# Expert tiles of a mixture-of-experts layer: SyncE reads the row numbers of four pairs of tiles at once

## The reference

```python
x = x + xattn(layernorm(x), ...)
h = layernorm(x)
probs = softmax(h @ router_weight.T)
topv, topi = top_k(probs, 4); topv = topv / sum(topv)
g = einsum('th,ehf->etf', h, w_gate)       # 32 experts, 256 -> 96
u = einsum('th,ehf->etf', h, w_up)
out = einsum('te,etf,efh->th', combine, silu(g) * u, w_down)
shared = silu(h @ sw_gate) * (h @ sw_up) @ sw_down   # 256 -> 512 -> 256
x = x + out + sigmoid(h @ sgate_w) * shared
```

## Time and profile before

| | us |
|---|---|
| three timed runs | 517.47, 515.96, 512.97 |
| their median | 515.96 |
| the profiled execution, its span | 667.5 |
| TensorE busy in the span | 574.4 (86%) |
| VectorE busy | 363.5 (54%) |
| ScalarE busy | 288.7 (43%) |
| GpSimd busy | 269.4 (40%) |
| start of SP's first read of `tile_row` | 302.9 |
| start of the last transfer to `loaded` | 566.2 |

### The profile page before, as it was taken

The page is one execution under the profiler, slowest core; times in us unless marked ns, Lnnn a source line. Parts: engine busy times, 40 slices in busy tenths (PEclk is TensorE's granted clock), DMA queues, the critical chain, the costliest instruction groups (busy, mean ns, idle before and its releaser), DMA issues. The chain is left out here.

```text
span 667.5 us, 13365 instructions
## 1 busy us (share of the span) xinstructions
PE 574.4 (86%) x3945; PEld 478.3 (72%) x3945; DVE 363.5 (54%) x1199; ACT 288.7 (43%) x719; POOL 269.4 (40%) x344
## 2 busy tenths in 40 slices
PE   8998787788887777899998988778877898979998
PEld 7997777677777565677886666656666676658886
DVE  5575455555555351565553635445454444536998
ACT  5775444555444440613463545444454544401111
POOL 1004444445555458380034544445454454560000
PEclk9999788987778788699997977988989978989999
DMA  5573544444433322293145444544444544228996
GB/s 160 181 227 128 170 156 129 144 134 145 138 123 113 110 76 107 70 244 98 31 130 148 131 140 124 140 136 139 130 140 140 150 131 132 87 86 330 368 340 230
DMA packets 65956, 100.77 MB, mean 151 GB/s; under 512 B 9856, under 2 KB 52864, under 8 KB 65792
## 3 DMA queue, kind: packets, MB, share of 16 engines
q1 hardware_dynamic: 48704, 60.30, 30.6%
q0 software_dynamic: 12672, 35.41, 14.7%
q10 hardware_dynamic: 4512, 4.23, 1.9%
HBM read 55.92 MB, written 43.97 MB: 150 GB/s over the span
## 5 line engine op out<-in xcount | busy, mean ns | idle before, releaser
L512 POOL DMA_INDIRECT returned<-arena,back x136 | 130.6, 960 | 171.7 <-DVE back L1629 81.5
L481 POOL DMA_INDIRECT sent<-rows,slot x128 | 129.9, 1015 | 159.2 <-issue 82.7
L1100 PE MATMUL bank<-w_gu,arena 128*128 x416 | 94.7, 363 | 26.6 <-issue 16.6
L1100 PEld LDWEIGHTS bank<-w_gu,arena 128*128 128x128 f32 x416 | 73.0, 205 | 32.8 <-issue 32.8
L1580 DVE TENSOR_TENSOR arena<-bank,arena 128x192 f32<-128x192 f32 x68 | 24.2, 356 | 113.5 <-ACT arena L737 94.5
L737 ACT ACTIVATE arena<-bank 128x192 f32<-128x192 f32 x68 | 22.3, 329 | 127.0 <-remote 70.5
L806 PE MATMUL bank<-w_hi_all,att_split 128*128 128x256 f32 x256 | 56.8, 314 | 18.6 <-issue 18.6
L1597 DVE TENSOR_SCALAR arena<-bank,back_to 128x256 f32<-128x256 f32 x136 | 59.0, 476 | 6.3 <-remote 5.3
L806 PE MATMUL bank<-att_split,w_hi_all 128*128 128x256 f32 x256 | 55.5, 336 | 1.4 <-issue 1.3
L710 ACT COPY hnt<-w_gu 128x384 f32 x128 | 55.7, 509 | 0.0
L806 PEld LDWEIGHTS bank<-w_hi_all,att_split 128*128 128x128 f32 x256 | 42.4, 208 | 18.2 <-issue 18.2
(11 more groups left out here) (216 smaller groups left out, 1128.6 us busy)
## 6 DMA issues: line engine op xcount, KB each, us to landing
arena<-returned SPq DMA_DIRECT2D x16, 1024.0 KB, 7.2
loaded<-sent SPq DMA_DIRECT2D x104, 134.0 KB
w_gu<-w_gate_up SPq DMA_DIRECT2D x32, 192.0 KB
sent<-rows SPq DMA_DIRECT2D x4, 1072.0 KB, 6.2
loaded<-sent SPq DMA_DIRECT2D x128, 33.5 KB
resid<-x SPq DMA_DIRECT2D x16, 256.0 KB, 2.9
att_plain<-ctx_t SPq DMA_DIRECT2D x16, 256.0 KB, 3.1
out<-resid ACTq DMA_DIRECT2D x7, 512.0 KB, 4.9
```

The lines of the kernel that those rows point to most:

```text
L481: pool.indirect_dma_start(out=sent, out_offset=bass.IndirectOffsetOnAxis(ap=slot[:, 2 * b + j, k:k + 1], axis=0), in_=rows[:, u, j, :], in ...
L512: pool.indirect_dma_start(out=returned, out_offset=bass.IndirectOffsetOnAxis(ap=back[:, t:t + 1], axis=0), in_=down_e[u][:, s, :], in_offs ...
L1100: last = pe.matmul(view[:, s, :], rows_t[:, s, c, :], w_gu[:, c, bass.ds(e[s - 2 + len(e)], 1), :] .rearrange("p e f -> p (e f)"), start=( ...
```

## The change

SP reads at pairs 0, 4, 8 and so on with one instruction the row numbers of that pair and the three behind it: eleven values at pairs 0 and 64, fourteen at the others. Seventeen reads in place of 68. The registers are kept until their pairs' transfers are issued. The transfers, their waits and their order stay. The bound given to the compiler for the value, which is used for no check at run time, is now the same for all pairs.

```diff
             for pair in range(pairs):
-                u = pair % RING
-                first, size = column_of(pair), QUARTER if mixed(pair) else P
-                _, at = nc.values_load_multi_w_load_instructions(
-                    tile_row[0:1, first:first + (5 if mixed(pair) else 2)], engines=[mybir.EngineType.SP],
-                    min_val=0, max_val=EXPERTS * tokens - size,
-                    skip_runtime_bounds_check_because="a tile's first row is a row of an expert's "
-                                                      "region, at most its count less a tile on")
+                u, size = pair % RING, QUARTER if mixed(pair) else P
+                if pair % 4 == 0:
+                    first = column_of(pair)
+                    _, rows_at = nc.values_load_multi_w_load_instructions(
+                        tile_row[0:1, first:first + sum(5 if mixed(p) else 2 for p in range(pair, pair + 4))],
+                        engines=[mybir.EngineType.SP], min_val=0, max_val=EXPERTS * tokens - QUARTER,
+                        skip_runtime_bounds_check_because="a tile's first row is a row of an expert's "
+                                                          "region, at most its count less a tile on")
+                at = rows_at[column_of(pair) - first:]
                 wait(sp, "turned_psum", pair - RING + 1)
                 wait(sp, "back_ready", (pair - RING) // 2 + 1)
                 for q in range(P // size):
```

## The result

| | before | after |
|---|---|---|
| median of 11 runs each, us | 515.96 | 511.17 |
| lowest to highest, us | 510.08 to 519.54 | 510.09 to 512.86 |
| ratio, 95% interval | | 0.9917 (0.9889 to 0.9945) |

The change makes the kernel faster by 0.8% (4.3 us by the ratio, 4.8 us between the medians). That is less than 1%, but the interval of the ratio leaves out 1. The fastest runs of the two are equal, but on the side of the kernel before this is one run of 11; the next is 512.97. In a later set none of its 19 runs is under 513.43 us, and the changed kernel's eight are at 510.31 to 513.22.

The account below looks back on a forecast made before the run. TensorE was taken to bound the stage of 68 expert pairs, with SP's reads hidden by its lead; 0 us removed and 0 us added on the path left 516 us at 516, range 511 to 521.

Parts of the forecast that it names:

- within 1%: Whole kernel: timed result less than about 1%, 5 us, from no change; chance 0.85.
- The price of a read: SP's queue: 200 ns a value, 69 ns fixed, about half from columns divisible by four; reads 46.9 us before, 46.5 after.
- SP's load is equal and under TensorE's: Expert stage, four pairs: SP 10.4 to 11.0 us before, 10.8 after; TensorE 12.2 us.
- The clean stretch is the hardest on SP: Expert stage, 336.7 to 352 us: TensorE sets the pace, 3.06 us a pair, leaving SP least time; model of timed runs.
- some four pairs: Ring of six tiles: SP is this far ahead of TensorE, which hides later transfers; without it, 29 us.
- the half with the read: SP, two of four pairs: 6.6 us against 6.1 for two pairs, so pair 4k at most 0.5 us behind its release.
- The 42.2 us of waiting of SP: SP waits for DVE's slot lists at L1629, 18 times: the supplier waits for its customers, not they for it.
- The first rival, a late pair 4k: Long read makes pair 4k late, TensorE waits at L1049 once in four pairs; 524 us, up to 545; chance 0.08.
- The second rival, tiles that come earlier: Reads have a fixed price, tiles come earlier: 513 us, or 506 to 509 with unseen waits; gain over 1%: chance 0.08.

Follow-up runs that it names:

- aligned8: The changed kernel with groups of eight pairs beginning at pairs 7, 15, 23 and a first group of seven, 9 reads; 510.97 us, 0.9887 of the kernel before.
- first trace: Profile of the unchanged kernel before that the prediction used, at the slow level; it spans 667.5 us.
- second trace: New profile of the unchanged kernel before, at the 515 us level; it spans 512.7 us, timed median 514.98 us.
- four_at_once: Kernel before with its 68 reads kept, those of four pairs one behind the other ahead of pair 4k; 512.61 us, ratio 0.9916.
- warm80b: Kernel before with 80 warming transposes on TensorE at the very start in place of 16; 524.34 us.
- groups of two: The change with two pairs to a read in place of four, 34 reads; 510.99 us, ratio 0.9889 to the kernel before.

## Why the prediction was wrong

The forecast was 516 us and no change; measured were 511.17 us and a gain of 0.8%. That the time still lies in the range, at its lower edge, and that "within 1%", held at 0.85, came true, is luck as far as the mechanism goes: the forecast had SP's queue off the path, and it was on it. Its own numbers already allowed that.

- **The price of a read: right in its balance, low in its sum.** 46.9 us before and 46.5 after were forecast, 53.4 and 52.3 us measured: the balance of the two is right to a microsecond, each sum is some 6 us too low. The read of fourteen was put at 2.87 us; the first two take 2.89 and 2.88, and the 13 from 256 us on 3.02 to 3.51. The Trainium skill, "DMA: Bandwidth & Descriptors", section "Latency and other measured facts", gives a `tensor_load` a floor of about 600 ns; by an estimate from it 31 us of reads would have gone. The traces disagree, 1.1 us went. That a read from a column divisible by four is cheaper was right: 28 values take 1.66 to 2.03 us.
- **"SP's load is equal and under TensorE's": the step that failed.** It set SP's 10.4 to 11.0 us for four pairs against TensorE's 12.2. At the 515 us level it is 11.81 for SP (pairs 8 to 64, first transfer to first transfer) and, where SP doesn't hold it up, 11.44 for TensorE (aligned8). Two terms were mis-sized in opposite directions, and they crossed. TensorE's is 0.8 us too high. It came from pairs 6 to 10 of the first trace (12.25 us), and one step of these, from pair 8 to 9, takes 3.88 us there (342.45 to 346.33 in the earlier trace rows), against 2.68 for the next one; in the second trace that step takes 3.01 us, and all four 11.37. SP's is 0.8 to 1.4 us too low. It came from undisturbed durations: the issues of the transfers sum to 12 us more than at their median durations, 0.7 us for four pairs, and the reads to 6.5 us more than forecast, 0.4 for four pairs.
- **"The clean stretch is the hardest on SP": wrong.** In that trace SP had issued pair 0's transfers 20 us ahead of their use (303.79 and 324.27), in the second trace 6 us ahead. In the first trace the time from a pair's last transfer to its use is never under 6.0 us, at pair 8 it is 7.0 (335.41 to 342.45): a little over two pairs of 3.06 us, and not the "some four pairs" of the forecast. At pair 8 the second trace has 4.2 us, at pair 39 2.2. A queue that is 3% too slow loses about 0.1 us a pair, so that a few pairs with a lead can't show it. The forecast's own sum, too, gives the half with the read as 6.8 us (3.4 + 0.5 + 2.87) and not 6.6; nothing hung on that.
- **The 42.2 us of waiting of SP: misread.** They were the slack of an execution whose pairs take 3.97 us. In the stretch from 329.9 to 352 us of that same trace, in which the forecast saw its model of a timed run, SP waited only once:

```profile
SPq L265 <- DVE back L1629: 1.1, 1, 1.1
```

  The forecast noted 29% between the profiled and the timed execution and took that off TensorE's side alone.
- **The first rival, a late pair 4k:** not in the changed kernel; once, for 1.3 us, in four_at_once, at pair 8, where the lead is short.
- **The second rival, tiles that come earlier:** right in its direction, too large in its size (506 to 509 us) and wrong in its cause. It needed waits for tiles that the first trace did not show, and they were there. But no price by instruction was saved. SP's queue, first read to last transfer, fell from 193.3 to 185.1 us, and of these 8.2 us the reads give 1.1. The quarter transfers give 10.7, the whole ones take back 2.0, gaps between instructions give some 2, and 3.7 us are new waiting. 4 us of it reach the end; then TensorE sets the pace.

Why the quarter transfers got shorter is read off the traces. Of the 15 fetches of q8 that began while SP was at the transfers, SP was 0.3 us after their start in the issue of a transfer in 9 cases in the second trace of the kernel before (7 quarters, 2 whole) and in a read in none. After the change it was in a read in 9 cases, in the second run of it again in 9, and in four_at_once in 8. A long read is lengthened by a fetch by 0.2 us on average, less than such reads differ among themselves: the nine in the changed kernel took 2.88 to 3.51 us, mean 3.27, the other four long enough to compare (of fourteen values, without a fetch of q8 or q14) 2.89 to 3.21, mean 3.07. So a read of 3 us at the right place of the four pairs takes in, for 0.2 us, a fetch that costs a transfer about 0.8. That the place of the reads does it and not their number is shown (four_at_once), and that the long transfers follow the fetch (warm80b). In groups of two SP was in a read in only 2 of the 15 cases, and 11 of the whole tiles' transfers take over 0.45 us. There the sums give 10.8 us less on quarter transfers, 6.8 more on whole ones and 4.0 less on reads. So to cover fetches by long reads is the changed kernel's way to the 8 us, not the only one. What sets the phase of the two to each other, and why it differs from run to run of the kernel before, wasn't tried. That it makes the spread, 9.5 us before and 2.8 us after, is a guess.

## What to carry to other kernels

Hold a queue's whole load for a period, fetches and gaps included, against the period of the engine it feeds, on a trace that took as long as the timed runs; a profiled execution 29% longer hid a queue that was 3% too slow. If a queue is that near, look at how the lead from issue to use changes over the stage, not at the margin of one pair. And price reads of registers by value and by the first column: making them fewer saved 1.1 of 53 us here (the groups of four gave up eight cheap first columns for it), putting them together saved more, by where they then stood when instructions were fetched.

## What the hardware showed that was not expected

- The issue of a transfer takes 0.32 to 0.35 us on SP. When an instruction fetch of queue q8 has started in the last 0.4 us, it takes 0.87 to 1.75 us in two cases of three (43 of 65) (1.16 at 317.2, 1.68 at 293.3 above); a read of fourteen values is 0.2 us longer on average with one inside it. In the stage of the kernel before long issues cost some 12 us of SP's 193: 53.1 + 36.9 us against 78 us at median durations.
- Reads of registers: 200 ns a value beyond the second (469 ns for two, 1069 for five); fourteen values from an odd column take 2.88 to 3.51 us. From a column divisible by four, four values come to 0.27 us (542 ns for five, less the fifth and the fixed 69 ns), and 28 values take 1.66 to 2.03 us, 1.90 on average.
- The same kernel takes about 515 us in some sets of runs and 644 to 678 us in others, on one chip both. In the first trace, of the latter kind, there are stretches like the earlier trace rows at 352 us, in which SP's instructions stand 0.7 us apart. What makes them wasn't found.
